# Cross-attention and a small feed-forward layer: x turned by VectorE, its norm left out of the query projection, and the last sums on TensorE

## The reference

```python
# x: (2, 2048, 512); context: (2, 128, 512); 16 heads of 32 columns; all fp32
a = layernorm(x)                                   # over 512 columns, eps 1e-5
q, k, v = a @ Wq, ctx @ Wk, ctx @ Wv               # split into heads
q, k = layernorm(q) * gq + bq, layernorm(k) * gk + bk     # over the 32 columns of a head
x = x + softmax(q @ k.T / sqrt(32)) @ v @ Wo
s = layernorm(x) @ Win + bin                       # 64 columns
h = relu(s[..., None] * W1 + b1)                   # 16 hidden units for each column
x = x + ((h * W2).sum(-1) + b2) @ Wout + bout
```

## Time and profile before

| | us |
|---|---|
| median of 3 runs | 462.93 |
| lowest, highest | 462.91, 463.62 |
| span of the profiled execution, first to last instruction | 461.9 |
| PE busy (share of the span) | 425.7 (92%) |
| DVE busy | 332.5 (72%) |
| ACT busy | 322.7 (70%) |
| POOL busy | 247.2 (54%) |

### The profile page before, as it was taken

One profiled execution on the slowest core, in us unless ns is written; L12 is line 12 of the kernel. 1 busy time (PEld: TensorE's weight loads), 2 busy tenths in 40 slices (PEclk: granted clock), 3 DMA queues, 4 the chain that ended last, 5 costly groups with the idle time before them and its releaser, 6 DMA issues.

```text
span 461.9 us, 7732 instructions
## 1 busy us (share of the span) xinstructions
PE 425.7 (92%) x2328; PEld 283.8 (61%) x2328; DVE 332.5 (72%) x646; ACT 322.7 (70%) x623; POOL 247.2 (54%) x330
## 2 busy tenths in 40 slices
PE   4999989999999999999999999999978996899942
PEld 2567767476577748774767567765754572367721
DVE  4987986584478956897488946874798466555886
ACT  3669757977649982999469974986299549763650
POOL 4557977365733674377535625645373422144773
PEclk9999999999999999999999999999997999799975
DMA  8564894934840387208911592038600981151004
GB/s 293 150 199 130 202 221 97 197 107 107 213 114 28 70 247 185 70 26 240 225 37 51 159 242 57 4 90 238 130 4 0 248 178 35 45 175 55 1 1 182
DMA packets 25289, 58.34 MB, mean 126 GB/s; under 512 B 5920, under 2 KB 6432, under 8 KB 22176
## 3 DMA queue, kind: packets, MB, share of 16 engines
q1 hardware_dynamic: 24992, 57.58, 47.6%
q10 hardware_dynamic: 256, 0.26, 0.2%
HBM read 22.18 MB, written 8.39 MB: 66 GB/s over the span
## 4 chain that ended last, share of the span: by engine, by line
PE 67%; DVE 9%; SPq 7%; issue 6%; ACT 5%; DMA 3%; POOL 2%; DVEq 0%; ACTq 0%; POOLq 0%
PE bank L1988 31%; PE bank L2084 8%; PE bank L2072 7%; PE bank L1994 6%; DVE bank L922 5%; PE bank L2051 5%; PE bank L2087 4%; SPq L359 3%; PE bank L2152 3%; PE bank L2137 2%; DMA q_stack<-qt_hi 1%; PE bank L2096 1%; ACT hid L1502 1%; DMA xin<-in_x_dram 1%; POOL u L561 1%
## 5 line engine op out<-in xcount | busy, mean ns | idle before, releaser
L838 DVE TENSOR_REDUCE mx<-bank 128x4 f32<-128x512 f32 x128 | 83.3, 684 | 24.4 <-PE bank L2051 24.3
L1420 ACT ACTIVATE prob<-bank 128x512 f32<-128x512 f32 x128 | 71.7, 601 | 29.0 <-PE bank L2072 24.3
L1502 ACT ACTIVATE hid<-s_in,b_col,w_col 128x256 f32<-128x256 f32 x118 | 63.4, 598 | 4.3 <-DVE s_in L891 3.4
L2084 PE MATMUL bank<-prob,v_kv 128*32 128x512 f32 x256 | 65.6, 622 | 0.0
L2087 PE MATMUL bank<-prob,den_sel 128*32 128x512 f32 x256 | 65.0, 622 | 0.0
L922 DVE SCALAR_TENSOR_TENSOR bank<-hid,w_col,bank 128x256 f32<-128x256 f32 x120 | 58.1, 485 | 7.7 <-ACT hid L1502 0.5
L568 POOL TENSOR_TENSOR qt_lo<-u,qt_hi 128x512 fp32r<-128x512 f32 x32 | 41.2, 1294 | 30.2 <-ACT u L1397 30.1
L556 POOL TENSOR_TENSOR squares<-u 128x512 f32<-128x512 f32 x32 | 33.2, 1041 | 39.7 <-ACT u L1378 39.2
L1988 PE MATMUL bank<-wq_hi,zt_hi 128*128 128x512 f32 x128 | 52.8, 413 | 1.2 <-DVE zt_lo L825 1.0
L589 POOL TENSOR_TENSOR x<-x,bout_row 128x512 f32<-128x512 f32 x28 | 35.8, 1285 | 33.8 <-PE bank L1994 17.1
L2072 PE MATMUL bank<-q_stack,k_stack 97*128 97x512 f32 x128 | 47.1, 436 | 6.4 <-DMA q_stack<-mxt 2.6
(11 more groups left out here) (171 smaller groups left out, 912.3 us busy)
## 6 DMA issues: line engine op xcount, KB each, us to landing
q_stack<-qt_hi SPq DMA_DIRECT2D x64, 256.0 KB, 4.6
xin<-in_x_dram SPq DMA_DIRECT2D x36, 256.0 KB, 3.4
q_stack<-qt_lo SPq DMA_DIRECT2D x32, 256.0 KB, 4.8
x<-in_x_dram SPq DMA_DIRECT2D x28, 256.0 KB, 4.3
out_dram<-x SPq DMA_DIRECT2D x28, 256.0 KB, 2.5
att<-in_L_xattn_Wk_dram SPq DMA_DIRECT2D x1, 1024.0 KB, 6.4
x<-in_L_xattn_Wq_dram SPq DMA_DIRECT2D x4, 256.0 KB, 7.1
hid<-in_L_xattn_Wv_dram SPq DMA_DIRECT2D x1, 1024.0 KB, 9.5
```

The source lines that it names most:

```text
L838: dve.tensor_reduce(mx[:, j, :].rearrange("p (g i) -> p i g", g=G)[:, 2 * half + r, :], maxs_banks[T][half][j][r][:, :].rearrange("p (g n) ...
L1420: act.activation(prob[:, h % PR, :], score_bank[t][h][:, :], ACT.Exp, scale=SCALE).then_inc(exp_done, 1)
L1502: act.activation(hid[:, hh % RR, :], of_half(s_in), ACT.Relu, bias=b1_col[:, hh:hh + 1], scale=w1_col[:, hh:hh + 1]).then_inc(hid_done, 1)
L2084: pe.matmul(at_bank[t][c][rows(n), :], v_kv[kv_of(t)][:, n * HD:(n + 1) * HD], prob[:, n % PR, :], start=True, stop=True)
```

## The change

**x.** `z1_norm`, `newton1`, `guess1` and `turn_z1` are gone. SP loads x with eight transfers for a block in pieces of 512 bytes, so that 32x32 squares lie where a square-wise transpose leaves a whole transpose (`load_x`, L456); DVE turns a tile in place (`turn_x`, L1119), ACT and, from block 3 on, POOL take the high and low part from SBUF (`z1_high`, `z1_low`); in blocks 0 to 2 DVE takes the low part. x is projected without its norm. The mean is removed through Wq, from which the mean of each column over all 512 rows is subtracted too (`sum_wq` on PE, `flatten_wq` on DVE); the scale cancels in the norm of each head, up to eps, which `add_eps` puts right with the variance of x. For that variance x is loaded a second time (`load_stats`, L462).

**Maxima.** DVE turns them in squares (`turn_max`); SP copies them with eight transfers (`stack_max`, L499). `turn_max` on PE and `move_max` on ACT are gone.

**Last units.** In blocks 6 and 7 units 4 to 15 are summed by PE: `sum_unit` (L2818) multiplies each with a diagonal matrix of its weights, built by DVE (`diagonal`). Units 9 to 12 are made by DVE, 13 to 15 by POOL. DVE adds units 0 to 3 in SBUF and then joins both sums.

**g.** The two parts of g have tiles of their own, no longer a corner of `at_hi` and `at_lo`; the waits of `att_high` on `y_done` go to `g_high`. `project_o(T, 0, 0)` waits for two low parts instead of four.

**Orders.** The written orders of all five engines and all bank tables are new, a row for each block; there is no repeated iteration.

```diff
@@ PE
-            def turn_z1(T, j):
-                pe.wait_ge(z1_done, T * TB + j + 1)
-                turn(z1_bank[T][j], columns(xin[:, j, :]), z1_turned)
+            def sum_wq():
+                pe.wait_ge(eyes, NEYES)
+                for c in range(C):
+                    pe.wait_ge(wq_centred, c + 1)
+                    ins = pe.matmul(wq_mean_bank[:, :], inv_d[:, :], wq_in[:, c, :], start=c == 0, stop=c == C - 1)
+                ins.then_inc(wq_summed, 1)
...
+            def sum_unit(T, hh):
...
+                pe.matmul(of_half(sum_bank[T]), diag[:, hh, :], hid[:, hh % RR, :], start=hh == SUMMED.start,
+                          stop=hh == HH - 1).then_inc(unit_summed, 1)
@@ DVE
+            def turn_x(T, j):
+                for g in range(G):
+                    dve.wait_ge(x_loaded[g][j // HT], T * 16 + 16)
+                dve.transpose(xin[:, j, :], xin[:, j, :]).then_inc(x_turned, 1)
+            def z1_low_early(T, j):
+                dve.wait_ge(zt_hi_done, T * TB + j + 1)
+                dve.tensor_tensor(zt_lo[:, j % 2, :, :].rearrange("p c (a s) -> p c a s", a=G), x_turned_of(j),
...
+            def flatten_wq(c):
+                dve.wait_ge(wq_summed, 1)
+                dve.tensor_tensor(wq_in[:, c, :], wq_in[:, c, :], wq_mean_bank[:, :], ALU.subtract).then_inc(wq_flat, 1)
+            def turn_max(T):
+                for half in range(2):
+                    dve.wait_ge(mx_done[half], (T + 1) * MAX_TILES)
+                if not first(T):
+                    dve.wait_ge(max_stacked, T * MAX_PARTS)
+                dve.transpose(mxt[:, :], mx[:, :].bitcast(F32)).then_inc(mx_turned, 1)
@@ SP
+            def load_x(T, half):
+                sp.wait_ge(zt_lo_done, T * TB - HT * (1 - half))
+                rows = slice(2 * G * half, 2 * G * (half + 1))
+                for g in range(G):
+                    sp.dma_start(x_parts[g][:, rows, :], x_by_part[T, g][:, rows, :]).then_inc(x_loaded[g][half], 16)
+            def load_stats(T, j):
+                if T * TB + j >= 2:
+                    sp.wait_ge(bn1_done, T * TB + j - 1)
+                sp.dma_start(xs[:, j % 2, :], x_t[T, j]).then_inc(xs_loaded[j], 16)
+            def stack_max(T):
+                sp.wait_ge(mx_turned, T + 1)
+                if not first(T):
+                    sp.wait_ge(scores_done, T * H)
...
+                for a in range(TB):
+                    for x in range(2):
+                        sp.dma_start(place_of[:, a, x].bitcast(F32),
+                                     mxt[32 * a:32 * (a + 1), 32 * x:32 * (x + 1)]).then_inc(max_stacked, 16)
@@ bank tables (one row of many)
-        z1_bank = banks_of([(4, 5, 6, 2)] + [(4, 7, 5, 7)] + [(2, 0, 3, 6)] + [(3, 1, 7, 3)] * 5)
```

More of the change, by code:

```diff
@@ L26 @@
 HT = TB // 2
-POOL_UNITS = range(2, HH, 3)
+LATE = 2
+EARLY = 3
+SUMMED = range(4, HH)
+MAX_FORM = range(9, HH)
+POOL_UNITS = range(13, HH)
 EPS = 1e-5
@@ L34 @@
 MAX_TILES = HC // 2 * TB
+MAX_PARTS = 16 * 2 * TB
 NEYES = 6
@@ L247, in first, with late, maker, units @@
             return t <= 0
-        def shared(t):
-            return t >= BLOCKS - 2
-        def act_units(t, hh):
-            if not shared(t):
-                return t * HH + hh
-            own = HH - len(POOL_UNITS)
-            return (BLOCKS - 2) * HH + (t - BLOCKS + 2) * own + len([n for n in range(hh) if n not in POOL_UNITS])
-        def pool_units(t, hh):
-            return (t - BLOCKS + 2) * len(POOL_UNITS) + len([n for n in POOL_UNITS if n < hh])
+        def late(t):
+            return t >= BLOCKS - LATE
+        def maker(t, hh):
+            if late(t) and hh in MAX_FORM:
+                return "pool" if hh in POOL_UNITS else "dve"
+            return "act"
+        def units(t, hh, engine):
+            before = [(b, n) for b in range(t) for n in range(HH)] + [(t, n) for n in range(hh)]
+            return len([1 for b, n in before if maker(b, n) == engine])
+        def on_pe(t, hh):
+            return late(t) and hh in SUMMED
+        def taken(t, hh, pe_takes):
+            before = [(b, n) for b in range(t) for n in range(HH)] + [(t, n) for n in range(hh)]
+            return len([1 for b, n in before if on_pe(b, n) == pe_takes])
+        def slot_free(engine, T, hh):
+            old = T * HH + hh - RR
+            if old >= 0:
+                t, n = divmod(old, HH)
+                engine.wait_ge(unit_summed if on_pe(t, n) else hsum_done, taken(t, n, on_pe(t, n)) + 1)
+        def s_of(t):
+            return rden[:, HT * P:] if last(t) else of_half(s_in)
+        def sum_of(t):
+            return of_half(rden) if last(t) else s_in[:, HT * P:]
         def of_half(a):
@@ L321, in load_wout @@
             def load_wout():
-                for part in range(2):
-                    sp.wait_ge(kv_projected[part], NB)
+                sp.wait_ge(kv_projected[0], NB)
                 for half in range(2):
```

3470 lines of the change are left out of this document (2214 added, 1256 removed), and 16 rows, old and new, of tables (maxs_rows, score_bank).

## The result

The changed kernel takes 466.7 us (465.3 to 468.34, 4 runs) against 462.9, 1.0084 times as long (95% interval 1.0059 to 1.0108). It is slower by 0.8%, and the prediction of 445, range 430 to 457, was wrong. It had given .06 to slower.

The account below looks back on a forecast made before the run. PE, busy 92% of the span, was taken as the bound in the middle. -18 + 2 + 7 - 9 - 1 + 1 = -18 on 461.9, plus 1.0: 445 us, range 430 to 457.

Parts of the forecast that it names:

- A: Transposes leave PE: 40 groups of four at .45 us each, 18.0 us saved (16.4 to 19.6).
- a turn at 47.1: Middle of the program: a turn of two blocks should fall from 49.3 to 47.1 us as transposes leave PE.
- B: The start: first query projection at 25 instead of 19.77, +2 us in all (-1 to +5).
- from 16.7 to 20.3: The start: `sum_wq` on PE directly behind the key products, 3.6 us for four products.
- C: The first scores: first score at 82 instead of 74.95, behind SP's small transfers, +7 us (0 to +11).
- which I put at 56: Ahead of the first scores: time of block 1's low part of x that frees SP's next load of x.
- The bound .68: Price of one 128x512 turn of x on DVE, bounded by an elementwise row of the same shape, .68 us.
- The estimate of 1.24: Alternative price of a 128x512 turn on DVE, 1.24 us, which would put the first scores up to 5 us later.
- D: The late stretches, 340:360 and 380:400: PE's new order fills gaps there, -9 us (-15 to 0).
- E: The tail: units summed on PE, `g_low` at 18 us after the last turns, -1 us (-3 to +9).
- F: The maxima inside the blocks: their path through DVE and SP barely covered by PE's other work, +1 us (0 to +5).
- The rival "slower": The eight small transfers of the maxima take SP 1.25 each, not .58: +6 in sum, 469 us; chance .06.

Follow-up runs that it names:

- the experiment: One group of four transposes put back on PE ahead of each of the 32 query projections of the changed kernel: 475.2 us, ratio 1.0266.

## Why the prediction was wrong, step by step

**A held where PE is the bound.** The price of a group, .45, is .52 by the experiment. The step assumed that nearly all groups stood where PE is the bound; in the changed kernel twelve of the 32 of x stand ahead of the first score, where PE waits. The sign that the prediction named, a turn at 47.1, shows little: by the steps of `project_y` the turns are 54.3, 48.6, 44.6 and 44.9 (183.78 to 376.23), since each block has an order of its own now. The four are 48.1 in the mean, against 48.8 for the same four before.

**B failed, +2 for +12.** The first projection is 15.5 us later (5.2 by the prediction), less 3.6 of values that have left. The step that failed is "from 16.7 to 20.3": it let `sum_wq` start when PE was free of the keys, and took the arrival of Wq to be that of before. The load had been rewritten with the change, and the text priced the arithmetic on Wq and never its transfer. Four loads with four outermost put the first projection 10 us later than sixteen loads with 32.

**C failed: 68.5 us for 57** from the first projection to the first score, 55.2 before. The form was right: from SP's load of x of block 2 on, the sum 9 x 1.25 + 7.0 + 4.6 + 2.7 = 25.6 is 26.5 in the trace, and PE does wait for the maxima, 2.17. The step that failed is "which I put at 56": the low part that frees this load ends at 77.17. These 21.2 us are the miss of the first score, 103.7 for 82. As an estimate from the traces they are made up of three things:

- 10.3 us: the first projection is later than 25 by as much (B).
- 4.4 us: the low part stands still beside POOL, 5.12 for .68. The prediction had put up to 1.17 on a low part with two SBUF inputs, the mean of two rows beside POOL instructions of 1.13. The length of such a stall goes by POOL's instruction, and the longest one in the start is 4.6. What the prediction tells from the Trainium skill ("SBUF — State Buffer", section "Who interferes with whom") is that the one that comes later waits in full. The rows 5.12 and 1.83 agree with it.
- the rest, 6.5 us: DVE's waits for the second copy of x, 6.9 in all, which the prediction put at nothing. No term has this copy, though it stands on SP behind the slower first loads (36.19, 39.77 and 49.50), and DVE needs it ahead of the low parts of block 1. That the two figures belong together is an estimate from the order of DVE's rows; the run that loads two tiles of the copy earlier shows 2.3 us at the first score.

PE's clock was lower too: behind the waits of 5.08 and 3.92 the granted clock is .50 in 59:62 and in 79:85, and .84 and .87 over 60:80 and 80:100, where PE had .9 or more in every slice up to 340 us before. Of the 35.6 us that PE is busy there, an estimate of 5 is due to it, a price that the prediction had only for the tail. How much of it reaches the first score is not shown, since SP sets that.

**A turn on DVE** takes .66 to .71, 32 of them:

```profile
L1119 DVE STREAM_TRANSPOSE xin<-xin x32: 661/698/712, 24.9 to 293.4; 128x512 f32<-128x512 f32 x32
```

The bound .68, taken from an elementwise row of the same shape, was right. The estimate of 1.24 was made from a figure of the Trainium skill for bf16 ("VectorE: DVE Perf Modes", section "The three transpose paths"). The trace does not agree with it for this shape and fp32.

**D was some -6 to -7 for -9.** The two late stretches have lost 8.2 us of their 9.5 of idle time, and with it the lower clock. But from the first score to the last turns PE's idle time fell only from 10.6 to 7.6 us, before and after (busy time, third column):

```profile
74.95:435.26 360.31, 349.69 (x1973) 229.67 (x1972) 251.74 (x487) 261.48 (x516) 178.32 (x233) 0.98 0.46 116
```

```profile
103.72:440.12 336.40, 328.76 (x1850) 215.97 (x1851) 257.44 (x518) 241.89 (x478) 192.62 (x215) 0.99 0.58 145
```

Other holes have opened, 2.4 us at 400:420 for one. The clock, .98 to .99 over this stretch, gives an estimate of 3 to 4 us more.

**E came to nothing** (-.1 for -1). The products of the units cost .45 at a clock of 1.00, as forecast. But `g_low` begins 19.4 us after the last turns (459.52 - 440.12) and not 18, where it was 19.1 before: PE's last sums wait 1.49 for DVE's diagonals and .44 for a unit from POOL. The last turns lie 26.5 us ahead of the end, 26.6 before.

```profile
459.52 0.41 DVE L1256 TENSOR_TENSOR g_lo<-bank,g_hi 128x256 fp32r<-128x256 f32 x1
```

**F held** (+1). The small transfers take .59, not 1.25:

```profile
L499 SPq DMA_DIRECT2D q_stack<-mxt x64: 519/591/1259, 97.4 to 387.1; - x64
```

PE waits for them 3.5 us in all, 2.2 of it at the first score. The rival "slower" rested on 1.25 and was wrong too: the kernel is slower for a reason that no rival held.

**The balance.** The miss of 21.7 us (466.7 against 445) is as large as that of the first score, 103.7 against 82. That the rest fits to a tenth (-23.9 behind the first score for -24) is in part luck. The -24 is what the milestones leave. By its terms the prediction has -20 there: -12 for the 27 groups of A that stand behind it, -9 and +1. And 82 holds C alone: with B (+2) and the thirteen groups of A ahead of it (-6) the same sum gives 78. The experiments price 9.0 us of the whole time in the layout of Wq's load (457.7 for 466.7), and then 4.3 in one POOL instruction, the second not clear of noise. The waits for the second copy of x were moved by several edits and never taken away whole, so their price in the time stays open.

## What to carry to other kernels

When a change rewrites how data lie, read every load again, its outermost dimension and its count, and not only the arithmetic; price the arrival of each operand before the first instruction that needs it. A start is a chain of several waits, each hidden by the one before: sum them on the new order, one by one, and take a removed wait as won only when the next one in the row is known. If an operand of DVE moves from PSUM to SBUF, look for the longest POOL instruction that can run beside it, not for the mean one, and cut that one. If an operand is loaded a second time, price where that load stands in its queue and what stands behind its reader.

## What the runs showed of the hardware

A load of 128 rows of 2 KB given as 4 x 32 kept the DMA engines at a share of .2 to .6. The same rows as sixteen loads of 32 brought them to .9, and the last quarter was there 10 us sooner, although SP issued four times as many. A DVE subtraction with two SBUF inputs, .68 alone, took 5.10 to 5.12 us beside a POOL instruction of 4.6 us that began .01 to .03 earlier (six traces of seven), and 1.83 when that was cut in four. In the seventh trace DVE took .68 and POOL's instruction 5.17. Cut in four, POOL's work took 5.50 for 4.60, with DVE's subtraction in between. A transpose in 32x32 squares of 128x512 in fp32 took DVE .70 us, about the price of a subtraction. Transfers of 4 KB into one partition took SP .59 us each.
